# Sixteen pairs of attention heads: a program with two loops, and the same program written out

## The chip, the cores and the metric

The kernel runs on one core of one Trainium2 chip. The metric is the device time of one execution in microseconds (us), the median of several runs. All arithmetic is in float32 or in its TensorE form float32r.

## The reference

The input x has 2 batches of 2048 tokens with 1024 channels. It is normalised by groups, goes through attention with 16 heads of 64 channels (8 heads look back, 8 look ahead), is projected by Wo and added to x:

```python
def _masked_attention(xf, Wq, Wk, Wv, lookahead):
    q = jnp.einsum('bnd,hed->bhne', xf, Wq)      # k, v alike
    s = jnp.einsum('bhqe,bhke->bhqk', q, k) * scale
    mask = i[:, None] <= i[None, :] if lookahead else i[:, None] >= i[None, :]
    s = jnp.where(mask, s, jnp.finfo(s.dtype).min)
    p = jax.nn.softmax(s, axis=-1)
    return jnp.einsum('bhqk,bhke->bhqe', p, v)
...
o_lb = _masked_attention(xf, Wq_lb, Wk_lb, Wv_lb, lookahead=False)
o_la = _masked_attention(xf, Wq_la, Wk_la, Wv_la, lookahead=True)
o = jnp.concatenate([o_lb, o_la], axis=1).reshape(B, T * F, D)
out = jnp.einsum('bnd,od->bno', o, Wo)
x = x + out        # _masked_attention was given _gn(x)
```

With two batches there are 2 x 16 = 32 heads to compute.

## The kernel before, in words

The kernel has two parts, one after the other. `project` normalises x and makes q, k and v of all heads as a high and a low half, which it stores in memory. It fills about the first 1170 us. The change does not touch it.

`attend` then computes the 32 heads as 16 pairs (`PAIRS`), p = 0 and p = 1 in each pair. A head is 40 tiles of scores, 128 keys by up to 512 queries. For each tile TensorE computes the scores (lines 996 to 1001), ScalarE takes the exponential twice (818 and 822), GpSimd or VectorE takes the low half as a difference (686), and TensorE multiplies by v three times (1015, 1017, 1019) into an accumulator. For the next head TensorE already computes scores whose row maxima VectorE reduces (968, then 889 and 894, with the mask added by 883). Of the head before, ScalarE copies the accumulator out (830), VectorE turns and inverts the sums and divides (916, 918, 923, 937), TensorE multiplies by Wo (1033), and VectorE adds the residual (950).

The order of all this work is a plan written out by hand. The function `slots` says which steps stand in each of the 40 slots of a head; every engine walks the same plan and picks its own steps. The engines are held together by semaphores alone, and every wait is on a count that is computed from the number of the pair, the head and the tile (`count`). There is no barrier between heads or pairs. The loads of the next head are issued by SyncE, which waits for tiles of the present head.

The function `pairs` (line 615) says how a program goes over the 16 pairs. It is called once for each of the five engines. Pairs 0, 7, 8 and 15 are written out. Pairs 1 to 6 are one body in a loop (line 618), pairs 9 to 14 are one body in another loop (line 622). `eng.Fori` is a loop of the engine itself: at its end the engine counts up a register, compares it and branches back. In a loop the number of the pair is a register, so a wait on a count is preceded by register instructions that compute the value (line 37); in a written-out pair the count is a constant. The two loops give 5 + 5 = 10 branches back on every engine.

What a pair computes is the same inside and outside a loop; only pair 0, which has no head before it and loads Wo, differs.

Of the kernel before, what the change touches and what calls it, by code (L numbers as in the profile page):

```python
# [20 lines left out]
LB, LA = 0, 1  # L21
# [412 lines left out]
PAIRS = G_HEADS // 2  # L434
# [102 lines left out]
def attend(nc, x_res, wo, qk_h, qk_l, v_h, v_l, out):  # L537
    with ExitStack() as ctx:
# [75 lines left out]

        def pairs(eng, body):

            body(0, LB, LB)
            with eng.Fori(1, PAIRS // 2 - 1) as i:
                body(i, LB, LB)
            body(PAIRS // 2 - 1, LB, LA)  # L620
            body(PAIRS // 2, LA, LA)
            with eng.Fori(PAIRS // 2 + 1, PAIRS - 1) as i:
                body(i, LA, LA)
            body(PAIRS - 1, LA, None)

        def heads(eng, do):

            for step, _, n in prologue():
                do(step, LB, 0, 0, n)

            def pair(i, kind, then):
                for p in range(2):
                    of = kind if p == 0 else then
                    following = (i, 1) if p == 0 else (i + 1, 0)
                    has_before = p == 1 or not isinstance(i, int) or i > 0
                    for step, later, n in slots(of is not None, has_before):
                        if later:
                            do(step, of, *following, n)
                        else:
                            do(step, kind, i, p, n)  # L640

            pairs(eng, pair)

            for step in ("leave", "invert", "spread", "divide"):
                do(step, LA, PAIRS, 0, 3)
            for part, half in ROUND_SLOT:
                do("round " + part, None, PAIRS, 0, half)
            for half in range(2):
                for n in range(12 * half, 12 * half + 12):
                    do("project", None, PAIRS, 0, n)  # L650
                do("add", None, PAIRS, 0, half)
# [53 lines left out]
        def _(sp):  # L705
# [36 lines left out]
            def pair(i, kind, then):  # L742
                for p in range(2):
# [13 lines left out]
                    if p == 1 or not isinstance(i, int) or i > 0:  # L757
                        before = 2 * i + (p - 1)
                        for half in range(2):
                            rows_out(before, half)  # L760
                            residual(before + 1, half)

            pairs(sp, pair)
            for half in range(2):
                rows_out(G_HEADS - 1, half)
# [314 lines left out]
```

## Time and profile before

| | |
|---|---|
| Median of 3 runs | 3290.93 us (3289.30 to 3291.39) |
| The profiled execution's own time | 3290.62 us |
| Its span in the trace | 3288.8 us |
| Mean granted TensorE clock | 0.983 |

The span runs from the first to the last instruction of the program; 1.8 us lie around it. In the timeline and in the chain of waits, the first number of a row is the time in us since the start of the span. PE is TensorE, PEld its weight loads, DVE VectorE, ACT ScalarE, POOL GpSimd, SP SyncE. A q behind the engine (DVEq) means its sequencer: instructions for registers, branches and waits, which do not count as busy.

### The profile page before, as it was taken

Reading aid. Unit: us, or ns where it says so; the run is one execution under the profiler, and the core shown is the slowest. Engines: PE = TensorE matmul, PEld = TensorE weight load, DVE = VectorE, ACT = ScalarE, POOL = GpSimd, SP = SyncE. Lnnn points to the kernel's source line nnn. Section 1 sums busy time; section 2 is a strip of 40 time slices with the busy share of each in tenths; the row PEclk is TensorE's granted clock in tenths of the full one; section 3 lists DMA queues with packets and bytes.
Section 4 is the critical chain, followed back from the end, with each engine's and each line's share of the span. In section 5 each row is a group of like instructions: output and inputs, shape, how many; then the busy total and the mean of one; then the engine's idle time right before and its main releaser. Section 6 shows DMA issues by size and latency. Waiting matters only on the chain.

```text
span 3288.8 us, 49072 instructions
## 1 busy us (share of the span) xinstructions
PE 3104.2 (94%) x14472; PEld 2510.5 (76%) x14472; DVE 1996.7 (61%) x3540; ACT 1591.7 (48%) x3173; POOL 1271.9 (39%) x996
## 2 busy tenths in 40 slices
PE   4999799799999969999999999999999999999998
PEld 3788688678888846777777777787777777777786
DVE  6222211421121168788878787887888788788875
ACT  2210111211121136666666666666666666666665
POOL 2000000200000045556556565655655565556554
PEclk9999899899999979999999999999999999999999
DMA  7546534553453464343334333433432343334330
GB/s 241 149 123 148 162 123 103 166 154 115 99 148 105 97 134 97 68 99 85 71 71 105 75 70 80 101 76 68 102 82 71 76 103 74 67 87 98 72 69 22
DMA packets 354509, 333.55 MB, mean 101 GB/s; under 512 B 276480, under 2 KB 276480, under 8 KB 342016
## 3 DMA queue, kind: packets, MB, share of 16 engines
q1 hardware_dynamic: 354304, 331.41, 40.5%
q8 instruction: 57, 0.93, 0.1%
q14 instruction: 148, 1.21, 0.1%
HBM read 213.91 MB, written 117.44 MB: 101 GB/s over the span
## 4 chain that ended last, share of the span: by engine, by line
PE 55%; DVE 7%; issue 2%; DMA 0%; ACT 0%; DVEq 0%; SPq 0%; ACTq 0%
PE rows L1033 11%; PE max L968 7%; PE scores L1001 7%; PE acc L1019 7%; PE acc L1015 7%; PE acc L1017 7%; PE scores L996 7%; DVE o_full L937 3%; DVE part_max L889 1%; PE scores L999 1%; PE side L978 1%; DVE inv L916 1%; DVE inv L923 1%; DVE max L883 0%; DVE wo_l L907 0%
## 5 line engine op out<-in xcount | busy, mean ns | idle before, releaser
L686 POOL TENSOR_TENSOR p_low<-probs,p_high 128x512 fp32r<-128x512 f32 (+2 forms) x960 | 1215.5, 1278 | 874.0 <-ACT p_high L822 801.5
L818 ACT ACTIVATE probs<-scores 128x512 f32<-128x512 f32 (+3 forms) x1280 | 683.9, 534 | 614.1 <-PE scores L1001 601.7
L889 DVE TENSOR_REDUCE part_max<-max 128x1 f32<-128x512 f32 (+3 forms) x1280 | 765.3, 602 | 196.6 <-PE max L968 176.6
L822 ACT ACTIVATE p_high<-scores 128x512 fp32r<-128x512 f32 (+3 forms) x1280 | 680.3, 531 | 0.0
L968 PE MATMUL max<-k,q 128*128 128x512 f32 (+3 forms) x1280 | 481.9, 377 | 79.4 <-DVE part_max L889 61.6
L326 DVE TENSOR_TENSOR stage_l<-proj,stage_h 128x512 fp32r<-128x512 f32 x192 | 132.3, 690 | 685.1 <-ACT stage_h L318 660.5
L318 ACT ACTIVATE stage_h<-proj 128x512 fp32r<-128x512 f32 x192 | 114.6, 598 | 805.8 <-PE proj L264 425.1
L1001 PE MATMUL scores<-q,k 128*128 128x512 f32 (+3 forms) x1280 | 488.4, 382 | 0.0
L996 PE MATMUL scores<-q,k 128*128 128x512 f32 (+3 forms) x1280 | 470.2, 367 | 0.3 <-ACT p_high L822 0.3
L1019 PE MATMUL acc<-p_low,v 128*128 128x512 f32 (+3 forms) x1280 | 468.3, 366 | 0.0
L1015 PE MATMUL acc<-p_high,v 128*128 128x512 f32 (+3 forms) x1280 | 465.9, 364 | 0.6 <-DVE p_low L686 0.6
L1017 PE MATMUL acc<-p_high,v 128*65 128x512 f32 (+3 forms) x1280 | 461.8, 361 | 0.0
L264 PE MATMUL proj<-xh,wh 128*128 128x512 f32 x896 | 351.8, 393 | 26.3 <-DVE wl L293 26.3
L968 PEld LDWEIGHTS max<-k,q 128*128 128x128 f32 x1280 | 244.0, 191 | 153.8 <-DVE part_max L889 99.5
L264 PE MATMUL proj<-xl,wh 128*128 128x512 f32 x896 | 351.2, 392 | 0.0
L264 PE MATMUL proj<-xh,wl 128*128 128x512 f32 x896 | 350.8, 391 | 0.0
L1019 PEld LDWEIGHTS acc<-p_low,v 128*128 128x128 f32 x1280 | 241.3, 189 | 91.1 <-issue 0.8
L207 POOL TENSOR_TENSOR xl<-xs,xh 128x1024 fp32r<-128x1024 f32 x16 | 42.1, 2636 | 616.0 <-ACT xh L368 616.0
L1015 PEld LDWEIGHTS acc<-p_high,v 128*128 128x128 f32 x1280 | 242.0, 189 | 44.2 <-DVE p_low L686 1.2
L996 PEld LDWEIGHTS scores<-q,k 128*128 128x128 f32 x1280 | 242.3, 189 | 36.7 <-ACT p_high L822 0.7
L1001 PEld LDWEIGHTS scores<-q,k 128*128 128x128 f32 x1280 | 242.4, 189 | 30.7
L937 DVE TENSOR_TENSOR o_full<-acc_s,inv 64x256 f32<-64x256 f32 x256 | 244.3, 954 | 1.8
(86 smaller groups left out, 4293.7 us busy)
## 6 DMA issues: line engine op xcount, KB each, us to landing
xs<-xT SPq DMA_DIRECT2D x64, 512.0 KB, 4.9
qk_h<-stage_h SPq DMA_DIRECT2D x128, 256.0 KB, 2.6
qk_l<-stage_l SPq DMA_DIRECT2D x128, 256.0 KB, 3.0
q<-qk_h SPq DMA_DIRECT2D x64, 512.0 KB, 4.9
k<-qk_h SPq DMA_DIRECT2D x64, 512.0 KB, 6.8
w_raw<-wqk SPq DMA_DIRECT2D x32, 512.0 KB, 4.0
v_h<-stage_h SPq DMA_DIRECT2D x64, 256.0 KB, 2.6
v_l<-stage_l SPq DMA_DIRECT2D x64, 256.0 KB, 3.1
```

The source lines that it names most:

```text
L264: last = nc.tensor.matmul(bank[4 * u + q][:, :], w[:, u, c, :], x[:, c, cols], start=(c == 0 and w is wh and x is xh), stop=(c == NC - 1 a ...
L686: eng.tensor_tensor(p_low[:, n % 4, part], probs[:, n % 4, part], p_high[:, n % 4, part].bitcast(F32), ALU.subtract).then_inc(done, 1)
L818: nc.scalar.activation(probs[:, n % 4, 0:cols], scores[n % 2][:, 0:cols], ACT.Exp, scale=SCALE).then_inc(exp_done, 1)
L822: nc.scalar.activation(p_high[:, n % 4, 0:cols], scores[n % 2][:, 0:cols], ACT.Exp, scale=SCALE).then_inc(high_act, 1)
L889: nc.vector.tensor_reduce(part_max[:, s % 2, at, m:m + 1], max_bank[n % 2][:, 0:cols], AX.X, ALU.max).then_inc(max_read, 1)
L968: nc.tensor.matmul(to[:, 0:cols], q1[:, p, qc * P:(qc + 1) * P], k1[:, p, key:key + cols], start=True, stop=True).then_inc(max_scored, 1)
L996: nc.tensor.matmul(to[:, 0:cols], k1[:, p, keys], q1[:, p, queries], start=True, stop=False)
L1001: nc.tensor.matmul(to[:, 0:cols], k2[:, p, keys], q2[:, p, queries], start=False, stop=True).then_inc(scored, 1)
L1015: nc.tensor.matmul(sums[:, col:col + cols], v[:, p, j, 0:P], high, start=first, stop=False, skip_group_check=True)
L1017: nc.tensor.matmul(sums[0:E + 1, col:col + cols], v[:, p, j, P:VC], high, start=False, stop=False, skip_group_check=True)
L1019: nc.tensor.matmul(sums[:, col:col + cols], v[:, p, j, 0:P], low, start=False, stop=final, skip_group_check=True).then_inc(weighed, 1)
L1033: last = nc.tensor.matmul(rows_bank[:, :], o[:, j, :], w[:, j, cols], start=(k == 0), stop=(k == 23))
```

## The change

Both loops go. The 16 pairs are written out in a row on every engine, with the number of the pair as a constant. The kind of head that follows is worked out from that number as it was given by hand before.

```diff
         def pairs(eng, body):
 
-            body(0, LB, LB)
-            with eng.Fori(1, PAIRS // 2 - 1) as i:
-                body(i, LB, LB)
-            body(PAIRS // 2 - 1, LB, LA)
-            body(PAIRS // 2, LA, LA)
-            with eng.Fori(PAIRS // 2 + 1, PAIRS - 1) as i:
-                body(i, LA, LA)
-            body(PAIRS - 1, LA, None)
+            for i in range(PAIRS):
+                after = i + 1 - (i + 1 == PAIRS)
+                body(i, LB if i < PAIRS // 2 else LA,
+                     None if i + 1 == PAIRS else LB if after < PAIRS // 2 else LA)
```

## Rows read from the trace of the kernel before

**Rows 1.** The page: span, and busy time of each engine with its share.
```profile
span 3288.8 us, 49072 instructions
PE 3104.2 (94%) x14472; PEld 2510.5 (76%) x14472; DVE 1996.7 (61%) x3540; ACT 1591.7 (48%) x3173; POOL 1271.9 (39%) x996
```

**Rows 2.** Stretches of one head: length; busy PE, PEld, DVE, ACT, POOL; clock, DMA, GB/s.
```profile
1464.60:1530.40 65.80, 63.31 (x309) 50.73 (x309) 52.91 (x100) 43.50 (x92) 37.69 (x31) 1.00 0.34 80
1530.40:1594.30 63.90, 62.83 (x309) 50.77 (x308) 52.30 (x97) 43.06 (x90) 37.86 (x31) 1.00 0.37 82
2177.20:2241.00 63.80, 62.72 (x309) 50.72 (x308) 52.52 (x99) 43.26 (x91) 38.05 (x31) 1.00 0.39 87
```

**Rows 3.** The chain that ended last: one division of every pair's second head (start, us, what).
```profile
1278.21 1.59 DVE o_full L937
...
1406.18 1.59 DVE o_full L937
...
2054.79 1.59 DVE o_full L937
...
2182.50 1.59 DVE o_full L937
...
2310.11 1.58 DVE o_full L937
...
2438.10 1.59 DVE o_full L937
...
3085.93 1.59 DVE o_full L937
...
3213.57 1.58 DVE o_full L937
```

**Rows 4.** The same chain: three of its ten pieces that are called issue.
```profile
1463.35 2.95 issue
...
1593.03 3.11 issue
...
3013.67 2.87 issue
```

**Rows 5.** Instructions of line 618, the first loop: duration ns min/median/max, first and last start.
```profile
L618 PEldq COMPARE_BRANCH  x6: 83/215/215, 1462.9 to 2111.5; - x6
...
L618 DVEq COMPARE_BRANCH  x6: 55/63/72, 1463.3 to 2111.9; - x6
```

**Rows 6.** Timeline around the first branch back: start, us, instruction, [idle before it <- releaser].
```profile
1466.41 0.30 DVE L883 TENSOR_TENSOR max<-max,beyond 128x128 f32<-128x128 f32 x1 [2.53 <-issue]
1466.53 0.28 ACT L818 ACTIVATE probs<-scores 128x128 f32<-128x128 f32 x1 [2.33 <-PE scores L1001]
...
1467.49 0.50 PE L968 MATMUL max<-k,q 128*128 128x512 f32 x1 [1.23 <-DVE part_max L889]
```

**Rows 7.** DMA queues that fetch instructions, 1464.0 to 2113.3 us (in the first loop).
```profile
q14 instruction: 50, 0.41, 0.2%
```

**Rows 8.** DMA queues that fetch instructions, 2113.3 to 2368.7 us (two written-out pairs).
```profile
q8 instruction: 10, 0.16, 0.3%
q14 instruction: 11, 0.09, 0.1%
```

**Rows 9.** Register instructions of the waits (line 37), in one looped head, 1400.8 to 1464.6 us.
```profile
L37 PEldq ALU_OP  x79: 32/32/36, 1401.1 to 1464.4; - x79
L37 ACTq ALU_OP  x40: 35/35/35, 1401.9 to 1463.5; - x40
```

## The prediction

> **What bounds the kernel now.** I read the page first. TensorE is busy for 3104.2 of 3288.8 us; VectorE, the next, for 1996.7 [rows 1]. So time can come only from TensorE's remaining idle time, or from what makes it idle. The change touches the second part of the kernel only, so next I cut that part into stretches of one head. In a head of a written-out pair TensorE is busy for 62.72 of 63.80 us; in the second head of a looped pair for 62.83 of 63.90; but in a first head of a looped pair for 63.31 of 65.80 [rows 2]. The granted clock is 1.00 in all three, which is the 2.4 GHz level, so the clock does not explain the longer head. Something stops TensorE once per looped pair.
>
> Then the chain of waits. In every head it passes the same division on VectorE, line 937. Taken at the second head of each pair, these starts are a clock that ticks once per pair [rows 3]. Its ticks:
>
> - pair 0 to 1, into the first loop: 1406.18 - 1278.21 = 127.97 us.
> - five ticks to pair 6, one branch back in each: 2054.79 - 1406.18 = 648.61 us, 129.72 each.
> - pair 6 to 7 and 7 to 8, both written out: 127.71 and 127.61 us.
> - pair 8 to 9, into the second loop: 2438.10 - 2310.11 = 127.99 us.
> - five ticks to pair 14, one branch back in each: 3085.93 - 2438.10 = 647.83 us, 129.57 each.
> - pair 14 to 15, written out: 127.64 us.
>
> The kernel before thus already holds the experiment: the same pair with and without a loop around it. A written-out pair takes (127.71 + 127.61 + 127.64) / 3 = 127.65 us.
>
> The same chain shows where the two microseconds go. At each of the ten branches back stands a piece called issue of about 3 us: time in which VectorE waited for nothing that the profile shows [rows 4]. The branch instruction itself takes 0.063 us on VectorE and 0.215 us on TensorE [rows 5]. After the branch at 1463.3 us VectorE is idle for 2.53 us and ScalarE for 2.33 us, although their inputs were there; TensorE has gone on meanwhile and then waits 1.23 us for a maximum of VectorE [rows 6]. This is the look of an engine whose next instructions are not there. Instruction fetches fit: in the loop the queue q8, with fetches of 16 KB (0.16 MB in 10), is silent, and q14, with 8 KB (0.41 MB in 50), makes 10 per pair [rows 7]. In the two written-out pairs q14 makes 11, half as many per pair, and q8 makes 10 [rows 8]. I read q8 as TensorE's, whose body of a pair stays on the engine, and q14 as that of the others, whose bodies do not. TensorE is not stalled by its own branch but by its partners.
>
> **The Trainium skill** agrees with this reading: "Runtime: NRT & Kernel Launch", section "Instruction fetch mechanics", says that engines other than TensorE hold two blocks of instructions, that fetching ahead is sequential, and that a taken branch to a block not held must wait for its fetch. It gives no price; the price above is from the rows.
>
> **The change, part by part.**
>
> Ten branches back go. Their price is what the five-and-five ticks cost beyond written-out pairs: 648.61 + 647.83 - 10 x 127.65 = 19.94 us. Part of this is the stall and part the register work of the waits, which the same pairs carry. The stall pieces alone are larger, about 2.95 us each, 29.5 us in ten [rows 4]. They are not the price, since TensorE works through tiles that it had ready for more than half of each: its wait in rows 6 is 1.23 us. I take the ticks, which measure the net effect.
>
> The two entries into loops go. 127.97 + 127.99 - 2 x 127.65 = 0.66 us. Those two pairs run from registers but come after no branch back, so this also prices the register work of a pair together with an entry: 0.33 us.
>
> The register instructions before waits go, 79 on TensorE's sequencer in a looped head at 32 ns and 40 on ScalarE's at 35 ns [rows 9]. They run beside the engine's queued work, which hides all but what is in the ticks already; I add nothing. Unhidden, TensorE's alone would be 79 x 0.032 = 2.5 us in each head, and the looped head of 63.90 us against 63.80 [rows 2] excludes that: 0.1 us shows.
>
> The exits from the loops are branches not taken; the pairs behind them are in my reference (127.71 and 127.64 us), so an exit costs under 0.1 us. Nothing.
>
> Nothing is moved: order of the steps on each engine, semaphores, tiles, and DMAs with their waits on SyncE's queue stay. No wait is added; waits on a register's value become waits on constants, as pairs 7, 8 and 15 have them. What is added is program: TensorE now fetches in every pair, 10 / 2 = 5 blocks [rows 8]. Ten more pairs (each loop's body was fetched once anyway) make 50 more fetches on q8, while q14 makes about half as many as before per looped pair. Their cost is inside the 127.65 us, since pairs 7 and 8 fetch just so; the largest of the three written-out ticks is 0.06 us above their mean. Both ends: a gain is excluded, a fetch speeds up nothing; at most the difference between written-out ticks, 0.1 us per pair, 1 us in all. I take 0. The cover is the fetch ahead while TensorE works.
>
> Sum: 19.94 + 0.66 = 20.6 us. The profiled execution took 3290.62 us (1.8 us around its span); less 20.6 this is 3270.0. The median of the runs is 0.3 us above the profiled execution, which is well inside the spread of 2.1 us.
>
> **The rivals.**
>
> *The entry's 0.33 us stays.* If what made pairs 1 and 9 longer is not the loop, the gain is ten times the difference to such a pair: 1296.44 - 10 x 127.98 = 16.6 us, and the time 3274.0. For it: the register work is hidden in most heads, and a change in the order of fetches could cost as much. Against: five ticks on each side agree to 0.1 us. 9 in 100.
>
> *The full stall comes back.* The chain shows about 29.5 us of issue time, and a reader of the chain alone would say 3290.6 - 29.5 = 3261. Against: ticks of written-out pairs, in which no such piece stands, are only 2 us shorter. It would take a long run of written-out pairs to drift faster than three single ones. 4 in 100.
>
> *Only the branch is saved.* If the idle time at a pair's end came from the work and not from the loop, the gain would be ten branches of 0.215 us [rows 5], 2.2 us: 3288.5, no difference that a measurement of this kernel can tell (I take 0.2%, 6.6 us, as that bound). The Trainium skill, "Advanced Engine Details and Errata", section "Control Flow Timing", prices a compare-and-branch at about 108 ns, which by itself would make 1.1 us of ten. The trace has 63 ns on one engine and 215 on another for the instruction, and 2.53 us of idle time behind it [rows 6]; whoever goes by the instruction's price misses that. Against this rival: the written-out pairs end without the extra time. 2 in 100.
>
> *Slower: TensorE starves for instructions.* With the loop, TensorE ran whole loops without a fetch; written out, it needs 50 more, one about every 25 us, beside the loads of heads. If a fetch came late each time and cost TensorE what a branch back costs a pair, 2 us, the kernel would take 50 x 2 - 20.6 = 79 us more: 3370. It decides from 20.6 / 50 = 0.41 us per fetch. For it: fetches and loads share the DMA engines. Against: four heads in a row, with ten such fetches and the same loads, run at 63.8 us each; at 0.41 us per fetch a written-out pair would be 2 us longer than it is. 2 in 100.
>
> **How the numbers follow.** The forecast has 83 in 100 and gives 3270.0. Its own range: the shortest written-out tick for all gives 0.5 us more gain, the spread of runs is 2.1 us, the unknown of the fetches 1 us. This reaches from 3267 to 3273; the first rival adds 3274, so the range is 3267.0 to 3274.5. Outside are the other rivals, 8 in 100, and some surprise in the sizes. Faster by over 0.2% hold the forecast and the first two rivals, 96 in 100; within it 2; slower 2.
>
> **What the profile after would show.** Right: ticks of line 937 of 127.6 to 127.7 us through all pairs from 1 to 15; no issue piece of 3 us in the chain; no branch in the second part; q8 with about 57 + 50 = 107 fetches; first and second heads alike, with TensorE busy for 62.7 of 63.8 us; the first part and the tail as before. A tick of 128 us would speak for the first rival; idle time of TensorE's weight loads by issue at intervals of 25 us for starving. The forecast is wrong if the first part moves, which nothing here makes it do, or if written-out pairs slow down when many stand in a row, which three single ones cannot rule out.

## The result and the profile after

The changed kernel takes 3265.85 us (median of 4 runs, 3261.99 to 3267.02), the kernel before in the same comparison 3291.16 us. The ratio is 0.9921, with a 95% interval from 0.9904 to 0.9938. It is 25.3 us faster; forecast were 20.6. The time lies 1.15 us below the range: the prediction was wrong, by a gain from a place that it had left out.

The page of the kernel after, span and busy time of each engine, answers to [rows 1]:

```profile
span 3263.4 us, 42402 instructions
PE 3095.6 (95%) x14472; PEld 2509.5 (77%) x14472; DVE 1996.6 (61%) x3540; ACT 1592.3 (49%) x3173; POOL 1277.8 (39%) x996
```

The work is the same by count (14472 products, 3540 instructions of VectorE), and 6670 register, branch and wait instructions are gone. Two heads in a row of a pair that was looped, as [rows 2] (stretch, length, busy PE, PEld, DVE, ACT, POOL, granted clock, DMA share, GB/s):

```profile
1457.60:1521.40 63.80, 62.69 (x310) 50.71 (x309) 52.55 (x99) 43.32 (x90) 38.11 (x30) 1.00 0.38 83
1521.40:1585.20 63.80, 62.72 (x310) 50.70 (x309) 52.47 (x99) 43.30 (x90) 38.10 (x30) 1.00 0.37 83
```

First and second heads are alike, and TensorE is idle for 1.1 us of each (63.80 less 62.69 or 62.72). The long head of 65.80 us is gone. The chain that ended last, the same division as in [rows 3] (line 933 now; start, us, what):

```profile
1273.48 1.59 DVE o_full L933
...
1401.18 1.59 DVE o_full L933
...
2039.54 1.59 DVE o_full L933
...
2167.20 1.59 DVE o_full L933
...
2294.79 1.59 DVE o_full L933
...
2422.45 1.59 DVE o_full L933
...
3188.31 1.59 DVE o_full L933
```

The ticks are 127.70, then 638.36 / 5 = 127.67, 127.66, 127.59, 127.66, and (3188.31 - 2422.45) / 6 = 127.64. All 15 together: 1914.83 us, 127.66 each, in place of 3213.57 - 1278.21 = 1935.36 [rows 3]. None of the ten issue pieces of [rows 4] is left in this chain. The fetches of instructions on the page, whole execution:

```profile
q8 instruction: 104, 1.70, 0.2%
q14 instruction: 93, 0.76, 0.1%
```

q8 makes 104 fetches, 47 more than the 57 of the kernel before (107 were forecast).

So the loops gave 20.5 us. The spans differ by 25.4 (3288.8 less 3263.4). Most of the rest is ahead of the loops. The timeline shows the first product of the second part, before and after (start, us, instruction, idle time before it):

```profile
1172.13 0.77 PE L968 MATMUL max<-k,q 128*128 128x128 f32 x2 [17.36 <-DMA k<-qk_l]
```

```profile
1165.07 0.76 PE L964 MATMUL max<-k,q 128*128 128x128 f32 x2 [17.35 <-DMA k<-qk_l]
```

The second part starts 7.1 us earlier, although the text of the first part is the same. In pair 0's first head, with the loads of Wo, 2.3 us are given back, so that the second head of pair 0 reaches its first product of p_low with v (line 1019, now 1015) 4.7 us earlier (1268.2 in place of 1272.9 us). 4.7 + 20.5 + 0.2 at the tail are the 25.4.

Where in the first part the 7.1 us arise can be read too. TensorE's waits there add up to 90.1 us before and 86.3 after. Most of the difference is one wait for weights (line 264; start, us, instruction, idle time), before and after:

```profile
383.83 0.79 PE L264 MATMUL proj<-xh,wh 128*128 128x512 f32 x1 [19.00 <-DVE wl L293]
```

```profile
378.86 0.79 PE L264 MATMUL proj<-xh,wh 128*128 128x512 f32 x1 [15.49 <-DVE wl L293]
```

The other 3 us are in busy time: TensorE's products of the first part take 1064.7 us before and 1061.3 after, at a mean granted clock of 0.97 and 0.98.

### The profile page after: what moved, and what is told of

Read it like the earlier page. It is cut to its first block, busy times and chain, and to the rows that moved or that the text cites. A ratio compares the mean times of both kernels' runs of the same rounds, so it can differ in the third digit from the quotient of the medians.

```text
span 3263.4 us, 42402 instructions
## 1 busy us (share of the span) xinstructions
PE 3095.6 (95%) x14472; PEld 2509.5 (77%) x14472; DVE 1996.6 (61%) x3540; ACT 1592.3 (49%) x3173; POOL 1277.8 (39%) x996
## 4 chain that ended last, share of the span: by engine, by line
PE 56%; DVE 7%; issue 1%; DMA 0%; ACT 0%; SPq 0%; DVEq 0%; ACTq 0%
PE rows L1029 11%; PE max L964 8%; PE scores L997 7%; PE acc L1015 7%; PE acc L1011 7%; PE acc L1013 7%; PE scores L992 7%; DVE o_full L933 3%; DVE part_max L885 2%; PE scores L995 1%; PE side L974 1%; DVE inv L912 1%; DVE inv L919 1%; DVE p_low L682 0%; DVE wo_l L903 0%
## 5 line engine op out<-in xcount | busy, mean ns | idle before, releaser
L964 PE MATMUL max<-k,q 128*128 128x512 f32 (+3 forms) x1280 | 480.3, 376 | 65.8 <-DVE part_max L885 48.0
```

What stands on the lines that cost most here:

```text
L964: nc.tensor.matmul(to[:, 0:cols], q1[:, p, qc * P:(qc + 1) * P], k1[:, p, key:key + cols], start=True, stop=True).then_inc(max_scored, 1)
```

## The experiments

Two questions: is the price of a branch back what the prediction says, and where do the 4.7 us come from? In all that follows, "the heads" is the time from the first product of p_low with v in pair 0's second head to that in pair 15's second head, and the table at the end gives the first of these two times; it holds all branches of the loops and nothing of the first part. "Start" is the start of the second part. "First load" is the time to landing of the first load of x for the second batch (line 157, at about 236 us). Mean packet times are those of the packets of 4096 bytes, the loads, between 215 and 345 us, averaged over the packet records of the trace.

**The same two kernels again**

> The kernel before, unchanged, a second time. What is open is that the changed kernel reaches the second part 7.1 us earlier (first row-maximum product at 1165.1 instead of 1172.1 us), though its first part is the same text. Theory A (each execution's first part differs by some us of its own): this profile shows that start anywhere from 1163 to 1175 us, and the runs scatter over several us. Theory B (the first part's time belongs to the program, by where its code or its arrays lie): the start is again 1171 to 1173 us. In both, a looped pair with a branch back ticks 129.6 us, a written-out pair 127.65.

> The changed kernel, unchanged, a second time. Theory A: the start of the second part is anywhere from 1163 to 1175 us, and with many runs the difference to the kernel before tends to 20.6 us. Theory B: the start is again 1164 to 1166 us and the difference stays at 24 to 26 us. In both, all pairs tick 127.65 us.

Measured: 3292.77 us and 3264.02 us. Starts 1173.5 and 1167.6; heads 1935.7 and 1914.9; first load 5.9 and 3.8 us (5.3 and 3.8 in the first profiles). The heads repeat to 0.3 us. The second head of pair 0 comes at 1274.4 and 1267.3 us, 7.0 us apart where the first two profiles have 4.7. The wait at line 264 is 19.5 and 15.6 us. The early start is no accident of one execution, and a second comparison gives the ratio 0.9918. But 2.5 us between two profiles of one program are its own scatter.

**The loops with a hint**

```diff
-            with eng.Fori(1, PAIRS // 2 - 1) as i:
+            with nc.Fori(1, PAIRS // 2 - 1, engines=[eng.engine], hint_back_edge=True) as i:
```

(and the second loop alike)

> Both loops stay; at the top of each turn every engine gets a hint that its branch back will be taken, so that the branch's target can be fetched before it. Theory 1 (the stall is a late fetch of instructions after a taken branch): the issue pieces of 3 us go, a looped pair ticks 128.0 us, and the kernel takes 3291 - 16.6 = 3274 to 3275 us. Rival (the stall is something else of the loop's end, as its register work or the branch itself): ticks stay at 129.6 us and the time at 3291.

Measured: 3280.18 us, ratio 0.9965 (0.9951 to 0.9979). The heads take 1925.4 us. Within the loops a first head takes 64.0 to 64.1 us instead of 65.7 and a second one 63.9 to 64.0: a tick of 128.0 as theory 1 said. The DMA queues from 1464 to 2095 us, well inside the first loop:

```profile
## 3 DMA queue, kind: packets, MB, share of 16 engines
q1 hardware_dynamic: 51552, 51.91, 37.7%
issues: line engine op xcount, KB each, median us to landing
```

No line of q8 or q14 stands between: not one instruction was fetched in these 631 us, against 50 fetches in the five pairs of [rows 7]. In the kernel before, half of a turn's ten fetches come right at the branch back (at 1593.0 us on VectorE); the queue from 1592 to 1598 us:

```profile
q14 instruction: 5, 0.04, 2.4%
```

Without these fetches there is no stall. This shows the stall to be the fetch behind the branch back. It shows one thing more: the same bodies, which in one turn execute 385 instructions on VectorE, 368 on ScalarE, 182 on GpSimd and 77 on SyncE, need no fetch at all when the branch is announced. So they are not too long to stay; what makes the engines fetch them again without a hint is not shown. The time is 5.7 us above the middle of the forecast, because 5.9 us were lost in the head behind the first loop, where the hint is wrong. The timeline there (start, us, instruction, idle time before it):

```profile
2124.27 0.25 DVE L918 RECIPROCAL inv_c<-inv 64x16 f32<-64x16 f32 x1 [5.29 <-issue]
...
2125.12 0.62 PE L968 MATMUL max<-k,q 128*128 128x384 f32 x1 [4.15 <-DVE part_max L889]
```

VectorE stands for 5.29 us and TensorE behind it for 4.15. It stands 16 us after its last branch of the loop (2103.0 us), and the first 8 KB fetch since 1414 us comes at 2121.9 us, while it stands: a late fetch again. That the wrong hint delayed it is likely but not shown; at the second loop's end the cost was 0.4.

**Whose branch is it?** The function `pairs` is called per engine, so one engine can be looped and another written out:

```diff
+            if eng.engine != mybir.EngineType.PE:
+                body(0, LB, LB)
+                with eng.Fori(1, PAIRS // 2 - 1) as i:
+                    body(i, LB, LB)
...
+            else:
+                for i in range(PAIRS):
...
```

pe_looped has == in place of !=.

> TensorE's program is written out, the other four engines keep both loops. Theory 1 (TensorE is stalled by its partners, whose bodies are fetched again after each branch back): the first head of a looped pair still takes 65.7 us, and pairs with a branch back tick 129.4 to 129.7. Rival (TensorE's own branch is part of the price): first heads take 64.5 us or less. Theory C (the first part is 4 to 5 us shorter where TensorE's program is the long one, by where code or arrays then lie): the second part starts at 1165 to 1169 us; if it goes with the other engines' programs, at 1171 to 1174. Time by theory 1 alone: 3291 - 1 = 3290; with C 3285.

> TensorE alone keeps both loops, with registers and branches back; the others are written out. Theory 1: no stall, first heads take 63.9 to 64.1 us, what is left is TensorE's own register work and its branch of 0.2 us, so a pair ticks 127.7 to 128.0 and the heads behind the first take together 1915 to 1919 us (1914.8 in the changed kernel, 1935.4 before). Rival: first heads of 65 us and more. Theory C: the second part starts at 1171 to 1174 us as before if TensorE's program decides, else at 1165 to 1169. Time: 3271 or 3266.

Measured: others_looped 3282.07 us, heads 1933.6, first heads 65.3 to 65.8. pe_looped 3271.95 us, heads 1916.0, first heads 63.8 to 63.9. A loop's end in others_looped (start, us, instruction, idle time before it):

```profile
1463.89 0.50 PE L974 MATMUL max<-k,q 128*128 128x512 f32 x1 [0.97 <-DVE part_max L895]
```

TensorE has no branch here and waits for VectorE all the same. Both fetch counts fit: q8 makes 104 and 57 fetches in the two, q14 148 and 93. Of the 20.5 us in the heads, TensorE's own loops hold 1.1 and those of the other four engines 18.8; 0.6 appear only with both. The forecasts were 3290 or 3285 us for others_looped, both too high, and 3271 or 3266 for pe_looped. And the first surprise about the first part: others_looped starts at 1166.2 with a first load of 3.9 us, as the changed kernel; pe_looped at 1171.2 with 5.4 us, as the kernel before. This was put down to the length of TensorE's program, as it turned out wrongly.

**Half the change**

```diff
-            body(0, LB, LB)
-            with eng.Fori(1, PAIRS // 2 - 1) as i:
-                body(i, LB, LB)
+            for i in range(PAIRS // 2 - 1):
+                body(i, LB, LB)
```

> Pairs 1 to 6 written out, the second loop kept: one half of the change. All theories: pairs 1 to 6 tick 127.67, pairs 9 to 14 as before (127.99 once, then 129.6), so the second part is 10.5 us shorter than before. Theory C: the start of the second part moves with the length of the program, to 1165 to 1174 us, in this run anywhere in it; time 3276 to 3281.

Measured: 3282.37 us (forecast 3276 to 3281), heads 1925.2, which is 10.2 less than before, where 10.5 were forecast; start 1175.3, first load 4.9 us. Half of the change has half of the loops' gain and none of the first part's.

**Fewer, larger turns**

```diff
-            with eng.Fori(1, PAIRS // 2 - 1) as i:
-                body(i, LB, LB)
+            with eng.Fori(0, 3) as m:
+                for u in range(2):
+                    body(2 * m + (1 + u), LB, LB)
```

> Both loops kept, but two pairs per turn and three turns each, so 4 branches back in place of 10, with the same register work. Theory 1 by count of branches: 4 x 1.7 + 12 x 0.3 = 10.4 us above the changed kernel's heads, 1925 us for the heads behind the first (1935.4 before). Rival (TensorE too now has a body that does not stay on its engine, 2 x 5 fetches of 16 KB, and its own branch back must wait for a fetch): a branch back costs 3 us or more, 1930 us and more.

Measured: 3301.59 us, slower than before (ratio 1.0031, 1.0020 to 1.0043); heads 1945.6. The rival holds, and more strongly than stated. The last head of each turn with a branch back takes 70.3, 72.0, 68.2 and 67.5 us, the next one 64.8 to 65.9. So a branch back costs 4.5 to 9.9 us, taking both heads together, not 1.7. Four dear ones are worse than ten cheap ones. The Trainium skill, "Runtime: NRT & Kernel Launch", section "Instruction fetch mechanics", gives TensorE room for 2048 instructions. By that rule a body of two pairs does not fit: it has 4 x 2 x 308 = 2464 products and weight loads, where one pair has 1232. The trace agrees: q8 fetched 122 blocks in all (57 before), and TensorE executes 2874 instructions in a turn (1449 with one pair).

**The first part's loops written out too**

```diff
-            with eng.Fori(1, turns) as m:
+            for m in range(1, turns):
                 for u in range(2):
                     body(2 * m + u, u, True)
```

> The changed kernel with the loops over blocks of the first part written out as well (the function blocks), so that the program has no branch back at all. Their bodies are small on VectorE and ScalarE. If branches back cost only where a body does not stay on its engine, the time is that of the changed kernel, 3266 within 2 us. If every branch back costs 1.7 us, eleven of them give 3266 - 19 = 3247 us. Theory B of the first part: with the code moved, the start of the second part may shift by several us either way and stay there in all runs.

Measured: 3266.62 us, heads 1914.7, start 1168.8. The first part has four loops with eleven turns in all, which makes seven branches back, not the eleven of the forecast; at 1.7 us each they would have given 12 us. They cost nothing that can be seen, and nothing was fetched again for them: q14 makes 94 fetches here and 93 in the changed kernel. A turn of these loops executes 396 instructions on TensorE and 30 to 60 on the others. Loops whose bodies are not fetched again cost nothing here.

**Why is the first part faster?** A load tells it most plainly. The chunk is the same, the queue ahead of it is the same (a store of qk_h and one of qk_l), and yet it lands after 5.3 us before and 3.8 us after. The loads of x from 215 to 345 us, in the view by tile:

Kernel before:

```profile
DMA to landing us min/median/max: 4.4/4.7/5.3
```

Changed kernel:

```profile
DMA to landing us min/median/max: 3.8/4.6/5.2
```

The first load is the slowest of the 16 before and the fastest after.

This load marks the difference; it does not make it. While the 16 loads run, TensorE does not wait at all: from 200 to 362 us its products keep one and the same distance between any two kernels, to 0.01 us. It waits behind them, at 384 us, for weights whose turn comes after the last load of x. The 16 loads are issued from 236.5 to 342.5 us before and from 235.0 to 337.8 after, and the 3.2 us between these lengths are nearly the 3.5 us of the wait at line 264. The two need not go together: after_longer, below, has a first load of 4.0 us and a wait of 19.2.

The packets of that one load take 373 ns on average before and 216 after. The mean packet of the eighth weight load takes 342 and 332 ns in the two profiles of the kernel before, 174 and 169 in those of the changed kernel: a pattern that seems to belong to the program. Theory C was that the programs' length decides where code and arrays lie in memory. First TensorE's program was made longer without executing more (6016 in place of 12032 in before_half):

```diff
             heads(pe, do)
+            with pe.register("never") as zero:
+                pe.reg_mov(zero, 0)
+                with pe.If(pe.snap(zero, min_val=0, max_val=1) == 1):
+                    for _ in range(12032):
+                        pe.wait_ge(consts, 5)
```

> The kernel before with 12,032 instructions of TensorE behind its last work, in a block that is jumped over: its program gets 47 blocks of 16 KB longer (as long as the changed kernel's) and nothing more is executed. Theory C (the length of TensorE's program alone moves the first part, by where code and arrays lie): the second part starts at 1165 to 1169 us in place of 1172 to 1173.5, packets of 4096 bytes between 215 and 345 us take 213 to 226 ns on average in place of 236 to 240, and the kernel takes 3286 us, give or take 2. Rival (something executed in the changed kernel does it): 1172 to 1174 us, 236 to 240 ns, 3291 us. The jump at the end may add up to 3 us in either.

> The same with 6,016 instructions jumped over, half the length. Theory C: some other pattern of packet times, as the kernel with the first loop alone written out had (234 ns, start at 1175 us); the start may lie on either side of 1172 us. Rival: 1172 to 1174 us and 236 to 240 ns.

Then two unused blocks were put in front of the array wqk, so that its weights are read from addresses 1 MB higher:

```diff
-                    load_w(wqk[n], n)
+                    load_w(wqk[n + 2], n)
...
-        "wqk": qk.transpose(0, 1, 4, 3, 2).reshape(BLOCKS, P, D),
+        "wqk": np.concatenate([np.zeros((2, P, D), np.float32), qk.transpose(0, 1, 4, 3, 2).reshape(BLOCKS, P, D)]),
```

> The kernel before with two unused blocks in front of the array wqk, so that its weights are read from addresses 1 MB higher and the arrays behind it may shift. Nothing else changes. Theory C1 (it is the place of the arrays in memory that counts): the mean packet time of single loads changes its pattern (the eighth weight load took 342 ns per packet in both profiles of the kernel before, 174 and 169 in those of the changed one), and the start of the second part may move by some us. Rival C2 (it is the place of the code alone): pattern and start as before, 1172 to 1174 us.

> The changed kernel with the same two unused blocks in front of wqk. Theory C1: the pattern changes and the start may leave 1165 to 1168 us. C2: 1165 to 1168 us again. In both the heads behind the first take 1914.8 us.

Measured: 3294.46, 3292.23, 3291.15 and 3266.40 us; starts 1176.8, 1174.5, 1174.8 and 1169.0. The pattern changed in three of the four (eighth weight load 254 ns in before_long, 211 and 313 in the shifted ones) and stayed in before_half (338), but the first load stayed at 5.3, 5.6 and 5.3 us in the three kernels from before and at 3.8 in after_shift. So the place of things moves single loads, but these moves alone do not make the gain. before_long was no test of the length that was meant, since two waits were packed into one instruction each and the addition came out at half. Hence again, with the right length (the difference to before_long), and with it on another engine:

```diff
-                    for _ in range(12032):
+                    for _ in range(24390):
```

> The kernel before with as much of TensorE's program jumped over at the end that it is as long as the changed kernel's to the instruction: 1,717,248 bytes. In the run before_long pairs of waits were packed into one instruction, so that its program had 1,321,792 bytes, not the length that was meant; 936,448 is that of the kernel before. Theory C (the length of TensorE's program decides where code and arrays lie, and that moves the first part): the second part starts at 1165 to 1169 us, the first load of the second batch takes 3.8 us in place of 5.3, packets of 4096 bytes between 215 and 345 us take 213 to 220 ns on average, and the kernel takes 3286 us, give or take 1.5. Rival (something executed in the changed kernel does it): 1172 to 1175 us, 5.3 us, 236 to 240 ns, 3291 to 3294 us.

> The changed kernel with the same block jumped over at the end of TensorE's program, 2,498,048 bytes. Theory C: the start of the second part is free to leave 1165 to 1169 us, to either side, as the place changes again; the heads behind the first stay at 1914.8 us, so the time moves with the start alone. Rival: 1165 to 1169 us and 3266 us.

> The kernel before with 780,800 bytes jumped over at the end of GpSimd's program in place of TensorE's. If the sum of all programs decides the place, the first part changes as in before_full. If TensorE's program alone does (in pe_looped the other four were 413 KB longer and the pattern of packet times stayed), start at 1172 to 1174 us and 236 to 240 ns as before.

Measured: before_full 3283.86 us (forecast 3286, give or take 1.5), ratio 0.9977 (0.9968 to 0.9987); pool_long 3281.41 us, ratio 0.9965 (0.9952 to 0.9979); after_longer 3266.55. The kernel before becomes 8 and 10 us faster by instructions that it never executes. The loads of x in before_full, same view and stretch:

```profile
DMA to landing us min/median/max: 4.0/4.5/5.7
```

```profile
1166.88 0.77 PE L968 MATMUL max<-k,q 128*128 128x128 f32 x2 [17.42 <-DMA k<-qk_l]
```

It starts at 1166.9 with a first load of 4.0 us, and its weight loads have the pattern of the changed kernel (eighth load 177 ns). pool_long starts at 1163.5 with 3.9 us, though TensorE's program is as short as before. So it is not TensorE's program alone that decides. The sum of all five fits every run so far. Last, two lengths in the gap that was left:

```diff
-                    for _ in range(24390):
-                        pool.wait_ge(consts, 5)
+                    for _ in range(23668):
+                        pool.wait_ge(consts, 5)
```

(and 20856 in sum_2020)

> As pool_long, with less jumped over at the end of GpSimd's program, so that the five engines' programs have 2,110,016 bytes together. So far every kernel with 1.35 to 1.92 MB together loads slowly in the first part, every one with 2.13 MB and more fast. Theory S (one threshold on the sum, as 2,097,152 would be): the first load of the second batch takes 3.8 to 4.0 us and the kernel 3281 to 3285 us. Rival (places shift smoothly, and the split so far is chance): 4.5 us and more, or 3288 us and more.

> The same with 2,020,032 bytes together. Theory S with a threshold between 2.02 and 2.11 MB: slow, 4.9 to 5.9 us for that load, 3290 to 3294 us. If fast, the threshold lies between 1.92 and 2.02 MB. Rival: something between the two.

Measured: 3283.73 and 3282.86 us, first load 4.1 and 3.8 us. Both load like the changed kernel: the threshold, if it is one, lies below 2.02 MB, and the guess of 2,097,152 was wrong. All kernels follow in order of the length of their programs as compiled. These lengths stand in no trace, but the fetches agree with them: the changed kernel, which executes nearly all of its program once, fetched 104 x 16,384 + 93 x 8,192 = 2,465,792 bytes of 2,493,824.

| Kernel | bytes, five engines | first load, us | pair 0's second head, us |
|---|---|---|---|
| before, before_again, before_shift | 1,352,064 | 5.3, 5.9, 5.3 | 1272.9, 1274.4, 1275.6 |
| hint | 1,352,704 | 5.9 | 1272.0 |
| before_half | 1,545,152 | 5.6 | 1274.8 |
| two_pairs | 1,661,568 | 5.1 | 1273.6 |
| pe_looped | 1,713,024 | 5.4 | 1271.6 |
| before_long | 1,737,664 | 5.3 | 1276.3 |
| first_out | 1,922,944 | 4.9 | 1275.8 |
| sum_2020 | 2,020,032 | 3.8 | 1272.1 |
| sum_2110 | 2,110,016 | 4.1 | 1265.6 |
| others_looped, before_full, pool_long | 2,132,864 to 2,133,120 | 3.9, 4.0, 3.9 | 1269.4, 1267.5, 1266.7 |
| after, after_again, after_shift | 2,493,824 | 3.8, 3.8, 3.8 | 1268.2, 1267.3, 1269.0 |
| all_out | 2,660,864 | 3.9 | 1269.5 |
| after_longer | 3,274,880 | 4.0 | 1268.7 |

The first load parts them without exception. So does the start of the second part: 1171.2 us and later in all nine kernels up to first_out, counting each profile, and 1169.0 and earlier in all ten from sum_2020 on. The arrival of pair 0's second head does too but for sum_2020, which starts at 1169.0 us and then loses 2.3 us in the first head, as the changed kernel did.

## Why the prediction was wrong, and where it was right

- **The price of the loops held.** Forecast: 19.94 us for ten branches back and 0.66 for two entries, 20.6. Measured in the heads: 20.5. The written-out tick was forecast at 127.65 and came out at 127.66. Three single pairs were enough to foretell twelve in a row.
- **The reading of the stall held, but for its reason.** The fetch behind the branch is shown by the hint, the partners' part by others_looped and pe_looped. What did not hold is that the partners' bodies do not stay on their engines: with the hint they stayed, with the same instructions in them. Reading 8 KB and 16 KB fetches as the others' and TensorE's fits with every run: q8 grows only where TensorE's program does.
- **Register work at nothing beyond the ticks held.** With the hint, looped pairs tick 128.0: about 0.3 us per pair are left for registers and the branch itself, the figure that the entries gave.
- **Fetches of TensorE at nothing held.** 47 more of them, and a tick 0.01 us longer than forecast.
- **The rivals.** The entry's 0.33 us did not stay, the full stall of 29.5 us did not come back, the branch's own price was a tenth of the gain, and TensorE did not starve.
- **The step that failed** is the sentence "The change touches the second part of the kernel only" together with "the forecast is wrong if the first part moves, which nothing here makes it do". The term was set to zero; it measured 4.7 us in the first two profiles and 7.0 in the repeats. What the prediction left out is that the edit also makes the programs longer, from 1.35 to 2.49 MB. before_full shows that more length brings such a gain by itself: it executes three instructions more than the kernel before (7.9 us between medians; 5.4 us at pair 0's second head, the rest in the heads, 1934.1 against 1935.4, and in the tail, 79.6 against 80.6). Between kernels that are all long, the change is worth about what was forecast: 3283.86 - 3266.55 = 17.3 us from before_full to after_longer, and 19.8 to after_again (3264.02), though none of these pairs has equal length to the byte (2.13 MB against 3.27 and 2.49).
- **The range** took in the bounds of the second part and the scatter of the runs. Added in full, 0.5 + 2.1 + 1, they reach down to 3266.4 us, so 3265.85 lies outside them too. It had no bound for the part that was not edited. That part's waits for loads, which the trace of the kernel before shows plainly, should have been one.

What stays open: why length does this. That it goes with where arrays lie was supported by the patterns of packet times, which changed when wqk was moved; but moving it did not bring or take the gain. What makes the loads of x take longer in the shorter programs was not found, nor what makes the engines fetch their bodies again when a branch back has no hint.

## What to carry to other kernels

In this kernel a branch back was free where nothing was fetched behind it, cost about 2 us per turn where the partners of the bounding engine fetched their bodies again, and 4.5 to 9.9 us where the bounding engine did too. Count the fetches per turn; the length of a body alone does not tell. Look for pieces called issue right behind a loop's branch, and price them with a written-out copy of the same body, not by their own length. When a change makes a program much longer or shorter, leave some tenths of a per cent of range for the parts that were not touched, and compare at equal length (a block that is jumped over) before all of it is credited to the edit.

## What was not expected of the hardware

Instructions that are never executed made this kernel 8 to 10 us faster: with 0.67 to 0.78 MB of them behind the last work of TensorE or GpSimd, 3282.9, 3283.7, 3283.9 and 3281.4 us in place of 3291.7. All kernels with up to 1.92 MB of programs waited 4.9 to 5.9 us for one certain load, all with 2.02 MB and more 3.8 to 4.1 us. A hint on a branch back removed every fetch from 630 us of a loop whose bodies were otherwise fetched again in each turn; the head behind one of the two loops then took 5.9 us longer.
